# Second pass over the adjacency matrix: units of 16 rows with 1 KB runs in place of 8 rows with 2 KB runs

## The chip, the core and the metric

One core of one Trainium2 chip runs the whole kernel. The metric is device time in microseconds for one execution; lower is better. The engines are TensorE (PE, matrix products), VectorE (DVE), ScalarE (ACT), GpSimd (POOL) and SyncE (SP, which here only issues DMAs). Sixteen DMA engines move data between HBM and SBUF (128 partitions); SP and ACT each have one hardware queue on all sixteen, called q1 (SP) and q10 (ACT) in the trace, and GpSimd has q0.

## The reference, cut to what matters

`x` is 8192 x 64, `adj` is 8192 x 8192 (256 MiB in float32), sparse in its values but stored densely.

```python
x = layernorm(x + 1 - 0.1 * x - 0.01 * sum(x * (adj @ x), axis=1))   # first layer
A = adj - diag(adj)
node_support = concat[(A > 0) @ h, (A < 0) @ h]                      # second layer, h = x
edge_output  = gru(node_support, h)
att          = softmax(where(A > 0, e_plus, where(A < 0, e_minus, NEG_INF)))
node_output  = gru((att * A) @ (h @ W), h)
x = layernorm(h + diag(adj) * edge_output + diag(adj) * node_output)
```

The attention logits depend on the row alone, so a row needs two sums over the matrix: `A @ h` and `(A > 0) @ h`, and the number of positive entries.

## The kernel before

The matrix is read twice. The **first pass** (class `First`, up to about 690 us) reads strips of 128 rows x 2048 columns with runs of 8 KB and computes the first layer. The **second pass** (class `Fast`) needs the matrix transposed, columns on the partitions, and is what the change touches. A third path, `Full`, runs only if a check of the signs at the end finds negative entries; with these inputs it does not run.

The second pass goes through K = 16 blocks of 512 rows. The 128 partitions are four groups of 32, and each group holds a quarter of the columns (2048), cut into 64 chunks of 32 columns. A block arrives in U = 8 units of 2 MB. A unit of the kernel before is 16 chunks (512 columns of each group, runs of 2 KB) x 256 of the 512 rows, so 8 rows on each partition; units 2w and 2w+1 are the two row halves of the same columns. Four units fit into `ring`. A unit takes four DMAs of 512 KB, one for each group: SP issues groups 0 and 1 (partitions 0 to 63), ACT issues groups 2 and 3 (`load_unit`, line 243).

For each unit POOL multiplies the diagonal of the block out (`no_diagonal`, L757, 256 elements on each partition). DVE then transposes 32 x 32 squares from `ring` into `at` (`turn`, L871). There are H = 16 transpositions in a block, each of 2048 elements on each partition, counted here from 0 to 15. One of them takes the 8 rows of eight chunks; numbers 0 and 2 read unit 0, numbers 1 and 3 read unit 1, numbers 4 and 6 unit 2, and so on. ACT makes the mask of each (`sign`, L998, `mask`<-`at`). PE multiplies in pairs: the weighed products of halves 2p and 2p+1 (`weigh`, L1078, reading `at`), then their mask products (`add`, L1090, reading `mask`); here a half is four chunks x 512 rows. So both transpositions and both masks of a pair must be there before its first product. `at` and `mask` hold two pairs.

Order on the queues. SP waits on the count of transpositions and then issues its two DMAs; `freed` (L257) gives the count: units 4, 5, 6, 7 are loaded after 3, 4, 7, 8 transpositions of the block, and units 0 to 3 of the next block after 11, 12, 15, 16. ACT issues its two DMAs behind the masks of halves 2, 3, 6, 7, 10, 11, 14, 15. Between SP's loads stands the store of an earlier block's result (L789, 128 KB in runs of 256 B); POOL loads 128 KB of rows in such runs in each block (L820).

Row-wise work for the block before is spread over the block: products on PE between the pairs (L1099 to L1138), gates and copies on ACT (L1008 to L1038), vector work on DVE (L878 to L952), and one power on POOL (L814), which stands ahead of the first unit's diagonal of the next block. ACT copies PE's sums out at the seam between blocks (L1008, L1009) behind the mask of half 0, and PE's first product of the block waits for that copy.

Of the kernel before, what the change touches and what calls it, by code (L numbers as in the profile page):

```python
# [5 lines left out]
P = 128  # L6
Q = 32
# [37 lines left out]
def build_gnn(nc, x, adj, w_gat, a_gat, w_ih_e, w_hh_e, b_ih_e, b_hh_e, w_ih_n, w_hh_n, b_ih_n, b_hh_n, out):  # L45
# [18 lines left out]
    UC = 16  # L64
    SLOTS = 4
    HC = 4
    RH = BANK // Q // 2
    U = 2 * (C // UC)
# [174 lines left out]
def load_unit(eng, b, prefix, k, v, groups=(0, 1, 2, 3)):  # L243


    RH, UC, GQ, slot = b["RH"], b["UC"], b["GQ"], v % b["SLOTS"]
    wide, rows = v // 2, v % 2
    raw = unit_view(b, slot).rearrange("p (f m) -> p f m", f=RH)
    for g in groups:
        eng.dma_start(  # L250
            raw[Q * g:Q * g + Q, :, :],
            b["adj"][bass.ds(k * BANK + rows * (RH * Q), RH * Q),
                     GQ * g + UC * Q * wide:GQ * g + UC * Q * (wide + 1)].rearrange(
                "(f ii) m -> ii f m", ii=Q)).then_inc(b["s_raw"][prefix][slot], 16)


def freed(v):  # L257


    return 4 * (v // 2) + v % 2 - 5  # L260
# [5 lines left out]


def pair_view(t, pair):

    at = 2 * (pair % 2)  # L270
    return t[:, at:at + 2, :, :].rearrange("p s c i -> p (s c) i")
# [477 lines left out]
def no_diagonal(nc, pool, b, prefix, k, u):  # L749

    U, UC, RH, SLOTS = b["U"], b["UC"], b["RH"], b["SLOTS"]
    start = (u % 2) * RH * Q
    raw = unit_view(b, u % SLOTS)[:, start:start + Q]
    diag = bass.AP(tensor=raw.tensor, offset=raw.offset, ap=[list(raw.ap[0]), [UC * Q + Q, RH], [1, Q]])
# [4 lines left out]
        in1=b["not_diag"][:, bass.ds(k + (U // 2 - 1 - u // 2), 1), :].to_broadcast([P, RH, Q]), op=ALU.mult)  # L759
# [6 lines left out]
class Fast:  # L766
# [15 lines left out]
    def sync(self, sp):  # L782
# [9 lines left out]
        def block(k, first, old):  # L792
            for u in range(slots if first else 0, U):

                sp.wait_ge(s["turned"], k * (2 * U) + freed(u))
# [51 lines left out]
    def vector(self, dve):  # L847
        nc, b, s, ps = self.nc, self.b, self.s, self.b["ps"]
        H, HC, RH = self.H, b["HC"], b["RH"]
# [9 lines left out]
        def turn(k, half, first):  # L859
            n = k * H + half  # L860
            pair, rows = half // 2, half % 2
            v = 2 * (pair // 2) + rows
# [6 lines left out]
            raw = unit_view(b, v % b["SLOTS"]).rearrange("p (f c q) -> p f c q", f=RH, q=Q)  # L869
            to = pair_view(b["at"], pair)[:, :, RH * Q * rows:RH * Q * (rows + 1)]  # L870
            nc.vector.transpose(  # L871
                to.rearrange("p c (f q) -> p f c q", q=Q),
# [650 lines left out]
```

## Time and profile before

| | us |
|---|---|
| median of 3 runs (1623.57 to 1632.53) | 1627.84 |
| the profiled execution | 1620.43 |
| its span, first to last instruction | 1618.8 |
| PE busy in the span | 1418.2 (88%) |
| DVE busy | 1375.8 (85%) |
| ACT busy | 1180.4 (73%) |
| POOL busy | 191.7 (12%) |

Times in the rows are counted from the start of the span. HBM delivered 543.56 MB in all, on average 338 GB/s. The mean granted TensorE clock was 0.977 of full speed. A line such as `L871 DVE STREAM_TRANSPOSE at<-ring` is line 871 of the kernel, its engine, its operation, and the tile written and read.

### The profile page before, as it was taken

The page shows a single profiled execution, that of the slowest core. Times are in us where ns is not written, and L with a number is a line of the kernel's source. Part 1 is how long each engine was busy: PE and PEld are TensorE (multiplying, and loading weights), DVE is VectorE, ACT ScalarE, POOL GpSimd, SP SyncE. Part 2 cuts the span into 40 slices and gives each one's busy share as a digit, 9 for nine tenths or more (in the row PEclk, how much of TensorE's full clock was granted, in tenths as well). Part 3 has the DMA queues.
Part 4 walks back from the last instruction along what each step waited for, and adds up shares of the span by engine and source line. Part 5 has one row for each costly group of instructions (what it writes and reads, how often), then busy time and mean ns, then how long its engine had stood idle before and what let it go on. Part 6 is the DMA issues. An engine that isn't in the chain of part 4 may idle for free.

```text
span 1618.8 us, 22381 instructions
## 1 busy us (share of the span) xinstructions
PE 1418.2 (88%) x6262; PEld 786.5 (49%) x6262; DVE 1375.8 (85%) x1335; ACT 1180.4 (73%) x1427; POOL 191.7 (12%) x243
## 2 busy tenths in 40 slices
PE   7988888888888888659999999999999999999995
PEld 6655555555555555424444444444444444444442
DVE  4999999999999999777878888888887888889883
ACT  5988888888888888656666667666666766676662
POOL 3001010101010101031111101110111111011100
PEclk9999999999999999979999999999999999999996
DMA  9999999999999999999999999999999999999970
GB/s 270 405 422 421 410 421 411 421 410 420 412 421 411 421 411 421 355 307 338 313 285 278 321 311 305 302 321 310 285 318 309 307 297 313 311 304 301 322 208 11
DMA packets 216970, 548.08 MB, mean 339 GB/s; under 512 B 52336, under 2 KB 52352, under 8 KB 184176
## 3 DMA queue, kind: packets, MB, share of 16 engines
q1 hardware_dynamic: 127280, 405.87, 70.0%
q10 hardware_dynamic: 88320, 138.95, 29.3%
q0 software_dynamic: 1344, 2.99, 0.7%
q14 instruction: 19, 0.16, 0.0%
q8 instruction: 7, 0.11, 0.0%
HBM read 543.56 MB, written 4.19 MB: 338 GB/s over the span
## 4 chain that ended last, share of the span: by engine, by line
PE 44%; DVE 21%; DMA 20%; issue 12%; ACT 1%; DVEq 1%; POOL 1%; ACTq 0%; SPq 0%; POOLq 0%
PE ps L1078 23%; DMA ring<-in_adj 20%; DVE ps L645 17%; PE ps L1090 12%; DVE at L871 3%; PE ps L607 2%; PE ps L1124 2%; PE ps L574 1%; PE ps L1129 1%; PE ps L1107 1%; PE ps L1119 1%; PE ps L1099 1%; PE ps L1114 1%; PE ps L1138 1%; ACT final L1009 0%
## 5 line engine op out<-in xcount | busy, mean ns | idle before, releaser
L998 ACT ACTIVATE mask<-at 128x2048 fp32r<-128x2048 uint32 x256 | 489.4, 1912 | 288.6 <-DVE at L871 287.2
L871 DVE STREAM_TRANSPOSE at<-ring 128x2048 f32<-128x2048 f32 x256 | 582.6, 2297 | 114.0 <-PE ps L1078 57.0
L607 PE MATMUL ps<-mask,parts 128*128 128x512 f32 x2048 | 543.1, 407 | 107.4 <-DVE ps L645 101.8
L645 DVE SCALAR_TENSOR_TENSOR ps<-ring,ps 128x2048 f32<-128x2048 f32 x256 | 585.8, 2299 | 51.6 <-DMA ring<-in_adj 34.8
L529 ACT ACTIVATE at<-ring 128x2048 bf16<-128x2048 f32 x256 | 489.2, 1911 | 92.4 <-DMA ring<-in_adj 87.6
L1078 PE MATMUL ps<-at,hk 128*64 128x512 f32 x2048 | 478.9, 604 | 56.5 <-ACT final L1009 30.0
L607 PEld LDWEIGHTS ps<-mask,parts 128*128 128x128 f32 x2048 | 366.0, 188 | 284.6 <-DVE ps L645 215.9
L1078 PEld LDWEIGHTS ps<-at,hk 128*64 128x64 f32 x2048 | 147.6, 138 | 306.2 <-issue 261.6
L1090 PE MATMUL ps<-mask,parts 128*128 128x512 f32 x1024 | 269.4, 405 | 5.9 <-issue 5.9
L1090 PEld LDWEIGHTS ps<-mask,parts 128*128 128x128 f32 x1024 | 182.3, 188 | 143.7 <-issue 103.1
L757 POOL TENSOR_TENSOR ring<-ring,not_diag 128x256 f32<-128x256 f32 x128 | 94.5, 738 | 551.1 <-DMA ring<-in_adj 550.7
L433 POOL TENSOR_TENSOR at<-at,lsum 128x512 f32<-128x512 f32 x7 | 7.3, 1045 | 430.9 <-DVE lsum L662 430.9
L998 ACT ACTIVATION_READ_ACCUMULATOR mask<-at (+1 forms) x256 | 47.8, 187 | 0.0
L529 ACT ACTIVATION_READ_ACCUMULATOR at<-ring 128x1 f32 x256 | 47.7, 186 | 0.0
L814 POOL TENSOR_TENSOR ls<-ls,power 128x4 f32<-128x4 f32 x16 | 16.5, 1033 | 232.2 <-DVE ls L947 232.2
L1124 PE MATMUL ps<-final,w_edge 128*64 128x512 f32 x64 | 36.1, 648 | 2.6 <-DVE final L911 2.6
L1125 PE MATMUL ps<-final,w_node 128*64 128x512 f32 x64 | 36.1, 648 | 0.0
L645 DVE DVE_READ_ACCUMULATOR ps<-ring,ps (+1 forms) x256 | 36.1, 141 | 0.0
L918 DVE SCALAR_TENSOR_TENSOR final<-final 128x512 f32<-128x512 f32 x16 | 11.1, 696 | 24.2 <-ACT final L1030 19.0
L621 DVE TENSOR_TENSOR mask<-ps,mask 64x512 fp32r<-64x512 f32 x16 | 11.1, 695 | 14.1 <-ACT mask L486 14.1
L574 PE MATMUL ps<-ident,final 128*64 128x128 f32 x256 | 17.1, 305 | 6.8 <-DMA final<-in_x 6.8
L1124 PEld LDWEIGHTS ps<-final,w_edge 128*64 128x64 f32 x64 | 6.4, 140 | 29.9 <-issue 25.7
(155 smaller groups left out, 669.2 us busy)
## 6 DMA issues: line engine op xcount, KB each, us to landing
ring<-in_adj SPq DMA_DIRECT2D x256, 1024.0 KB, 17.4
ring<-in_adj SPq DMA_DIRECT2D x256, 512.0 KB, 10.3
ring<-in_adj ACTq DMA_DIRECT2D x256, 512.0 KB, 11.8
stage<-h_rows POOLq DMA_DIRECT2D x16, 128.0 KB, 6.6
out<-final SPq DMA_DIRECT2D x16, 128.0 KB, 13.3
h_rows<-final ACTq DMA_DIRECT2D x7, 256.0 KB, 22.9
hk<-h_rows ACTq DMA_DIRECT2D x7, 256.0 KB, 23.9
final<-in_x ACTq DMA_DIRECT2D x2, 512.0 KB, 10.1
```

The lines of the kernel that those rows point to most:

```text
L529: nc.scalar.activation(signs[:, unit % 2, :], ring[:, unit % RING, :], ACT.Sign, accum_out=row_signs[:, unit:unit + 1]).then_inc(s["signs_ ...
L574: last = nc.tensor.matmul(ps[D * half:D * half + D, q % 4, P * i:P * i + P], xn[:, 4 * q + i, :], ident[:], start=True, stop=True, skip_gr ...
L607: last = nc.tensor.matmul(ps[:, 4 * (n % 2) + i, :], pair[:, t % 2, e, :], x2[:, cols], start=e == 0, stop=e == 1)
L645: nc.vector.scalar_tensor_tensor(out=gram, in0=ring[:, i % RING, :], scalar=1.0, in1=gram, op0=ALU.mult, op1=ALU.mult, accum_out=flat[:, b ...
L757: return nc.gpsimd.tensor_tensor(out=diag, in0=diag, in1=b["not_diag"][:, bass.ds(k + (U // 2 - 1 - u // 2), 1), :].to_broadcast([P, RH, Q ...
L814: nc.gpsimd.tensor_tensor(out=b["ls"][:, 3, :], in0=b["ls"][:, 2, :], in1=b["power"][:, 0:4], op=ALU.pow).then_inc(s["rstd_ready"], 1)
L871: nc.vector.transpose(to.rearrange("p c (f q) -> p f c q", q=Q), raw[:, :, 2 * HC * (pair % 2):2 * HC * (pair % 2 + 1), :]).then_inc(s["tu ...
L998: nc.scalar.activation(pair_view(b["mask"], half // 2)[:, :, cols], pair_view(b["at"], half // 2)[:, :, cols].bitcast(U32), ACT.Sign, accu ...
L1078: last = mm(o, h[:, c, :], b["at"][:, half % 4, cl, :], start=c < 2, stop=c >= H * HC - 2)
L1090: last = mm(ps[:, ACC_S, :], parts[:, c, :], b["mask"][:, half % MS, cl, :], start=c == 0, stop=c == H * HC - 1)
L1124: mm(ps[lo, bank, :], b["w_edge"][:, t, :], sums, start=True, stop=True)
L1125: mm(ps[hi, bank, :], b["w_node"][:, t, :], wsum, start=True, stop=True, skip_group_check=True).then_inc(s["gates"], 1)
```

## The change

A unit becomes 8 chunks (256 columns of each group, runs of 1 KB) x all 512 rows, so 16 rows on each partition. It is still 2 MB in four DMAs of 512 KB. A transposition takes 16 rows of four chunks, which is exactly one half of PE's products; numbers 2u and 2u+1 read unit u. SP loads units 4 to 7 after 2, 4, 6, 8 transpositions, and so on evenly; ACT behind each odd half. PE waits for one transposition (one mask) ahead of the products of a half, no longer for both of a pair. The buffers `at` and `mask` are freed half by half. The order of instructions on each engine is otherwise the same. `Full` is changed in the same way.

```diff
-    UC = 16
+    UC = 8
+    U = C // UC
-    HC = 4
-    RH = BANK // Q // 2
-    U = 2 * (C // UC)
+    HC = UC // 2
@@ load_unit
-    raw = unit_view(b, slot).rearrange("p (f m) -> p f m", f=RH)
+    raw = unit_view(b, slot).rearrange("p (f m) -> p f m", f=RB)
-            b["adj"][bass.ds(k * BANK + rows * (RH * Q), RH * Q),
-                     GQ * g + UC * Q * wide:GQ * g + UC * Q * (wide + 1)].rearrange(
+            b["adj"][bass.ds(k * BANK, BANK), GQ * g + UC * Q * u:GQ * g + UC * Q * (u + 1)].rearrange(
                 "(f ii) m -> ii f m", ii=Q)).then_inc(b["s_raw"][prefix][slot], 16)
-def freed(v):
-    return 4 * (v // 2) + v % 2 - 5
@@ no_diagonal
-    start = (u % 2) * RH * Q
-    diag = bass.AP(..., ap=[list(raw.ap[0]), [UC * Q + Q, RH], [1, Q]])
+    raw = unit_view(b, u % SLOTS)[:, (u % 2) * UC * (UC * Q):(u % 2 + 1) * UC * (UC * Q)]
+    diag = bass.AP(..., ap=[list(raw.ap[0]), [UC * Q + Q, UC], [1, Q]])
@@ Fast.sync
-                sp.wait_ge(s["turned"], k * (2 * U) + freed(u))
+                sp.wait_ge(s["turned"], k * (2 * U) + 2 * (u + 1 - slots))
@@ Fast.vector, turn
-            if pair % 2 == 0:
-                dve.wait_ge(s["diagonal_out"], k * self.U + v + 1)
+            if part == 0:
+                dve.wait_ge(s["diagonal_out"], k * self.U + u + 1)
-                dve.wait_ge(s["weighed_done"], n - rows - 2)
-                dve.wait_ge(s["mask_ready"], n - rows - 2)
+                dve.wait_ge(s["weighed_done"], n - 3)
+                dve.wait_ge(s["mask_ready"], n - 3)
-                to.rearrange("p c (f q) -> p f c q", q=Q),
-                raw[:, :, 2 * HC * (pair % 2):2 * HC * (pair % 2 + 1), :])
+                b["at"][:, half % 4, :, :].rearrange("p c (f q) -> p f c q", q=Q),
+                raw[:, :, HC * part:HC * part + HC, :])
@@ Fast.scalar, sign
-                act.wait_ge(s["added_done"], n - half % 2 - 2)
+                act.wait_ge(s["added_done"], n - MS + 1)
-            u = 2 * (half // 4 + 2) + half % 2
-            if half % 4 >= 2 and (u < U or not last):
+            u = half // 2 + SLOTS
+            if half % 2 == 1 and (u < U or not last):
                 load_unit(act, b, "f_", k + u // U, u % U, (2, 3))
@@ Fast.tensor
-            pe.wait_ge(s["turned"], k * H + half - half % 2 + 2)
+            pe.wait_ge(s["turned"], k * H + half + 1)
-            pe.wait_ge(s["mask_ready"], k * H + half - half % 2 + 2)
+            pe.wait_ge(s["mask_ready"], k * H + half + 1)
```

## Rows read from the trace of the kernel before

**Rows 1.** Chain of waits by time, 850 to 1600 us: start, length, what.
```profile
868.92 5.35 PE ps L1078 x16
...
925.28 3.65 PE ps L1078 x16
...
980.37 3.65 PE ps L1078 x16
...
1035.43 3.65 PE ps L1078 x16
```
**Rows 2.** Busy time by engine, one block; then granted clock, DMA share, GB/s.
```profile
980.37:1035.43 55.06, 52.55 (x246) 24.88 (x247) 46.47 (x47) 37.46 (x44) 7.67 (x10) 1.00 1.06 308
```
**Rows 3.** Timeline of the seam: start, length, engine, line, idle before, releaser.
```profile
1027.65 1.03 POOL L814 TENSOR_TENSOR ls<-ls,power 128x4 f32<-128x4 f32 x1 [13.98 <-DVE ls L947]
...
1029.59 2.31 DVE L871 STREAM_TRANSPOSE at<-ring 128x2048 f32<-128x2048 f32 x1 [2.02 <-PE ps L1078]
...
1034.72 0.58 ACT L1009 COPY final<-ps 64x512 f32<-64x512 f32 x1
```
**Rows 4.** The chain of waits, 700 to 1600 us, longest pieces.
```profile
745.69 17.56 DMA ring<-in_adj
774.19 15.20 DMA ring<-in_adj
...
813.79 21.18 DMA ring<-in_adj
```
**Rows 5.** Groups by line and shape: count, busy us, mean ns, idle before.
```profile
L871 DVE STREAM_TRANSPOSE at<-ring 128x2048 f32<-128x2048 f32 x203 | 462.6, 2298 | 79.9 <-PE ps L1078 52.6 <-POOL ring L757 22.5 <-ACT mask L998 3.0
L998 ACT ACTIVATE mask<-at 128x2048 fp32r<-128x2048 uint32 x203 | 388.1, 1912 | 225.1 <-DVE at L871 223.8
...
L757 POOL TENSOR_TENSOR ring<-ring,not_diag 128x256 f32<-128x256 f32 x101 | 74.2, 735 | 424.0 <-DMA ring<-in_adj 423.7
```
**Rows 6.** DMA in that block: packets by size, then each queue's share.
```profile
DMA packets 9247, 16.99 MB, mean 308 GB/s; under 512 B 1050, under 2 KB 1050, under 8 KB 9247
...
q1 hardware_dynamic: 4855, 8.47, 53.6%
q10 hardware_dynamic: 4344, 8.38, 51.3%
```
**Rows 7.** Busy time as in rows 2: 8 KB runs, 256 B, 2 KB, 2 KB, two blocks.
```profile
620.00:630.00 10.00, 8.40 (x34) 5.64 (x33) 9.87 (x11) 8.80 (x11) 2.69 (x2) 1.00 1.01 421
4.00:7.00 3.00, 0.21 (x2) 0.24 (x4) 0.00 (x0) 1.28 (x1) 3.00 (x6) 1.00 1.35 220
958.00:967.00 9.00, 9.00 (x46) 5.02 (x43) 8.37 (x6) 4.87 (x6) 0.74 (x1) 1.00 1.06 365
...
820.00:828.00 8.00, 8.00 (x48) 4.42 (x47) 7.40 (x14) 6.26 (x9) 0.74 (x1) 1.00 1.09 238
757.00:835.00 78.00, 73.87 (x358) 36.72 (x358) 61.64 (x67) 51.57 (x61) 10.35 (x13) 1.00 1.06 307
```
**Rows 8.** DMA queues from 990.7 to 994.1 us: packets, MB, share.
```profile
DMA packets 771, 0.85 MB, mean 246 GB/s; under 512 B 406, under 2 KB 406, under 8 KB 771
q10 hardware_dynamic: 387, 0.75, 93.1%
q1 hardware_dynamic: 384, 0.10, 17.4%
```
**Rows 9.** Timeline of the second pass's start.
```profile
697.21 4.53 POOL L459 TENSOR_TENSOR parts<-hk,parts 128x2048 fp32r<-128x2048 f32 x1
697.30 2.31 DVE L871 STREAM_TRANSPOSE at<-ring 128x2048 f32<-128x2048 f32 x1 [2.10 <-POOL ring L757]
...
701.69 0.72 POOL L757 TENSOR_TENSOR ring<-ring,not_diag 128x256 f32<-128x256 f32 x1
...
704.91 5.74 PE L1078 MATMUL ps<-at,hk 128*64 128x512 f32 x16 [25.53 <-DVE at L871]
```
**Rows 10.** Timeline of ACT: one ordinary DMA issue of 1024 packets, two slow ones.
```profile
661.23 0.34 ACTq L298 DMA_DIRECT2D hk<-h_rows  x1
...
675.08 3.16 ACTq L250 DMA_DIRECT2D ring<-in_adj  x1
...
688.94 2.60 ACTq L250 DMA_DIRECT2D ring<-in_adj  x1
```
**Rows 11.** Timeline: PE's first weighed products of blocks 1 and 2.
```profile
753.04 3.65 PE L1078 MATMUL ps<-at,hk 128*64 128x512 f32 x16 [1.02 <-DVE at L871]
...
809.62 3.65 PE L1078 MATMUL ps<-at,hk 128*64 128x512 f32 x16 [2.68 <-ACT final L1009]
```

More of the change, by code:

```diff
@@ L240, in _, with load_unit @@
                 full.vector(dve)
-def load_unit(eng, b, prefix, k, v, groups=(0, 1, 2, 3)):
-    RH, UC, GQ, slot = b["RH"], b["UC"], b["GQ"], v % b["SLOTS"]
-    wide, rows = v // 2, v % 2
-    raw = unit_view(b, slot).rearrange("p (f m) -> p f m", f=RH)
+def load_unit(eng, b, prefix, k, u, groups=(0, 1, 2, 3)):
+    RB, UC, GQ, slot = b["RB"], b["UC"], b["GQ"], u % b["SLOTS"]
+    raw = unit_view(b, slot).rearrange("p (f m) -> p f m", f=RB)
     for g in groups:
@@ L860, in turn @@
             n = k * H + half
-            pair, rows = half // 2, half % 2
-            v = 2 * (pair // 2) + rows
-            if pair % 2 == 0:
-                dve.wait_ge(s["diagonal_out"], k * self.U + v + 1)
+            u, part = half // 2, half % 2
+            if part == 0:
+                dve.wait_ge(s["diagonal_out"], k * self.U + u + 1)
             if not (first and half < 4):
-                dve.wait_ge(s["weighed_done"], n - rows - 2)
-                dve.wait_ge(s["mask_ready"], n - rows - 2)
-            raw = unit_view(b, v % b["SLOTS"]).rearrange("p (f c q) -> p f c q", f=RH, q=Q)
-            to = pair_view(b["at"], pair)[:, :, RH * Q * rows:RH * Q * (rows + 1)]
+                dve.wait_ge(s["weighed_done"], n - 3)
+                dve.wait_ge(s["mask_ready"], n - 3)
+            raw = unit_view(b, u % b["SLOTS"]).rearrange("p (f c q) -> p f c q", f=RB, q=Q)
             nc.vector.transpose(
-                to.rearrange("p c (f q) -> p f c q", q=Q),
-                raw[:, :, 2 * HC * (pair % 2):2 * HC * (pair % 2 + 1), :]).then_inc(s["turned"], 1)
+                b["at"][:, half % 4, :, :].rearrange("p c (f q) -> p f c q", q=Q),
+                raw[:, :, HC * part:HC * part + HC, :]).then_inc(s["turned"], 1)
         def weighed_sum(k, c):
@@ L993, in sign @@
             if not (first and half < MS):
-                act.wait_ge(s["added_done"], n - half % 2 - 2)
-            cols = slice(RH * Q * (half % 2), RH * Q * (half % 2 + 1))
+                act.wait_ge(s["added_done"], n - MS + 1)
             nc.scalar.activation(
-                pair_view(b["mask"], half // 2)[:, :, cols], pair_view(b["at"], half // 2)[:, :, cols].bitcast(U32),
-                ACT.Sign, accum_out=b["seen"][:, bass.ds(n, 1)]).then_inc(s["mask_ready"], 1)
-            u = 2 * (half // 4 + 2) + half % 2
-            if half % 4 >= 2 and (u < U or not last):
+                b["mask"][:, half % MS, :, :].rearrange("p c i -> p (c i)"),
+                b["at"][:, half % 4, :, :].rearrange("p c i -> p (c i)").bitcast(U32), ACT.Sign,
+                accum_out=b["seen"][:, bass.ds(n, 1)]).then_inc(s["mask_ready"], 1)
+            u = half // 2 + SLOTS
+            if half % 2 == 1 and (u < U or not last):
                 load_unit(act, b, "f_", k + u // U, u % U, (2, 3))
@@ L1191, in sync @@
             if u >= slots:
[L1192 removed]
+                sp.wait_ge(s["turned"], 2 * (u + 1 - slots))
             load_unit(sp, b, "g_", 0, u)
@@ L1218, in turn @@
             n = k * H + half
-            wide, part = half // 4, half % 4
+            u, part = half // 2, half % 2
             if part == 0:
-                dve.wait_ge(s["diagonal_out"], k * self.U + 2 * wide + 2)
-            raw = b["ring"][:, 4 * (wide % 2):4 * (wide % 2) + 4, :].rearrange("p r m -> p (r m)").rearrange(
-                "p (f c q) -> p f c q", f=RB, q=Q)
+                dve.wait_ge(s["diagonal_out"], k * self.U + u + 1)
+            raw = unit_view(b, u % b["SLOTS"]).rearrange("p (f c q) -> p f c q", f=RB, q=Q)
             nc.vector.transpose(
```

17 lines of the change are left out of this document (6 added, 11 removed).

## The prediction

> **What bounds the kernel now.** I read three views in this order: the chain of waits of the second pass, the busy time of one block, and the DMA queues in that block. The chain shows where the blocks begin: PE's first weighed products come at 925.28, 980.37 and 1035.43 us, so a block lasts 55.1 us [rows 1]. The block from 868.92 lasts 56.4, with products of 5.35 us for 3.65. In a block PE is busy 52.55 of 55.06 us, DVE 46.47, ACT 37.46 [rows 2]. PE sets the pace. The 2.5 us that it lacks stand at the seam: POOL's power at 1027.65 delays the diagonal, transposition 0 comes at 1029.59, the mask follows, ACT's copy ends at 1035.30 and PE starts at 1035.43 [rows 1, 3].
>
> The reader should see a second limit close behind. In blocks 0 to 2 the chain runs through loads of the ring, 17.6, 15.2 and 21.2 us long [rows 4]. From 757 to 835 us the DMA brought 307 GB/s and PE had 73.87 of 78 us of work [rows 7]. In the later blocks 308 GB/s suffice, because PE asks for no more [rows 2]. So DMA is within a few per cent of being the bound, and the change doubles the number of its packets.
>
> **The change, part by part.** The sum is made against the profiled execution, 1620.43 us (span 1618.8). The median of the three runs is 1627.84, 7.4 us more; I add my difference to the median.
>
> *Work of the engines.* The transpositions stay at 16 a block with 2048 elements on each partition, mean 2298 ns; the masks too, 1912 ns; POOL's diagonal keeps 256 elements, 735 ns [rows 5]. Only strides change. I cost these at nothing. DVE has 8.6 us free in a block [rows 2], that is 0.54 us for each transposition before it would matter; a cheaper stride gains nothing while PE or DMA is the bound. The DMA instructions stay at 16 a block on each queue; a DMA of 1024 packets was issued in 0.34 us [rows 10], so 512 packets in place of 256 cost no issue time by themselves.
>
> *Waits.* PE asks for one transposition instead of two. At the seam this gives nothing: PE waits there for ACT's copy (L1009) [rows 3], which stands behind the mask of half 0, transposition 0, POOL's diagonal and the power, all in the same order after the change. In the block PE hardly waits for a transposition. DVE may write into `at` one half earlier; of its 79.9 us of idle time from 850 to 1550 us, 52.6 are put down to PE [rows 5], but PE stays the slower engine, so this is slack. Loads get one transposition more of lead: unit 4 is released after 2 and needed by number 8 (before: 3 and 8), unit 5 after 4, needed by number 10 (before: 4 and 9). With 55.06 / 16 = 3.4 us for each, six periods of lead, 20.6 us, take the place of five, 17.2.
>
> *The start.* Transposition 1 no longer needs the second unit. It can follow number 0 (697.30, 2.31 us long) at 699.6; before, it waited for POOL's diagonal at 701.69 and came at 702.45. PE needs only number 0 and can start at about 699.7 for 704.91 [rows 9]. That is 5 us; the mask products behind it wait for POOL's low parts (L459), ready at 701.74, and that is covered by the 5.7 us of weighed products. I take -4.
>
> *Packets.* With 16 engines, the time from one packet to the next on an engine is 16 x size / rate. With both queues loaded the rows give: 256 B at 220 GB/s, 18.6 ns; 2 KB at 365 GB/s, 89.8 ns; 8 KB at 421 GB/s, 311 ns [rows 7]. No row shows 1 KB. A straight line from 256 B to 2 KB gives 18.6 + 768/1792 x 71.2 = 49.1 ns; the slope from 2 KB to 8 KB, (311.3 - 89.8) / 6144 x 1024 = 36.9 ns, leads back from 89.8 to 52.9 ns; the cheap end is half of 89.8, 44.9 ns, and the dear end is the whole 18.6 of a small packet on top of 36.9, 55.5 ns. I take 49.1, between its two neighbours, which is 334 GB/s.
>
> A block has 16384 packets of 1 KB, 1024 on each engine: 50.3 us (46.0 at the cheap end, 56.8 at the dear end). Its 1050 small packets [rows 6] add 66 x 18.6 ns = 1.2 us. Before, it was 512 x 89.8 ns = 46.0, and 1.2: 47.2 of 55.1 us. The other 7.9 us are lost where one queue has little to give and the rate falls to 238 GB/s [rows 7]. Such a stretch loses 1 - 238/365 = 35% of its time, so they are about 23 us of a block.
>
> How much of these stays decides. Two things shorten them: loads are released evenly and not two at a time, and the 256 B packets of the store hold up less. While the store is in SP's queue the two queues deliver packet for packet (384 and 387), so SP's queue brings 0.10 MB and ACT's 0.75 [rows 8]; with 1 KB packets the same number of turns moves half as much on ACT's side. At 334 GB/s a stretch of 238 loses 29%. If all 23 us stay, a block needs 50.3 + 1.2 + 6.6 = 58.1 us; if half of them stay, 54.8. I take the middle, 56.4 us, 1.3 over PE's 55.1. Two chains so near each other, coupled by three units, also wait for each other: from 757 to 835 us both PE (95% busy) and DMA ran near their limits [rows 7]. I put 0.5 us a block on that.
>
> *Sum.* Blocks 3 to 14 are twelve: 12 x (1.3 + 0.5) = 21.6 us; the last block prefetches nothing, 0.7. Blocks 0 to 2 were held by DMA already and keep their time, 0. The start gives -4. Together +18 us: 1638.7 for the profiled execution, 1646 for the median.
>
> *Two rules of the Trainium skill.* The 2 KB packets of this trace reach 365 GB/s where 8 KB reach 421 [rows 7]. "DMA: Bandwidth & Descriptors" (Specifications) puts the smallest transfer for full rate at 512 B, by which 1 KB would cost no more than 2 KB a byte; the rate of 2 KB speaks against it here, and by that rule the packets of a block stay at 46.0 us and the sum has no DMA term, which is the first two rivals below. "Advanced Engine Details and Errata" (Clock Domains) gives 42 to 43 ns for an unobstructed 1 KiB descriptor; as an estimate that is 43.5 us a block for the 50.3 above, and it too speaks against my slowdown. No row here shows a 1 KB packet.
>
> **The rivals.**
> *DMA keeps up, and nothing is won.* If half or more of the one-queue stretches go and 1 KB costs 49 ns or less, a block needs 54.8 us or less and PE's 55.1 stay. For it speaks the longer lead (20.6 for 17.2 us); against it, that blocks 1 and 2 were late with 2 KB [rows 4]. The start's gain is eaten in blocks 0 to 2, where loads are still the bound: 0 to +5 us, median 1630.
> *The other side: the release order was what held the early blocks.* Its place is blocks 0 to 2. Block 1 began at 753.04 us, block 2 at 809.62 [rows 11], block 3 at 868.92 [rows 1], so they lasted 56.6 and 59.3 us for 55.1. If even releases keep both queues filled, 1.5 + 4.2 = 5.7 us go there, and 4 at the start: -10 us, median 1618. It decides from the point at which a block's DMA work falls under 55 us in blocks 1 and 2 too. For it speaks that the rate is 365 whenever both queues give [rows 7].
> *Issues that block ACT.* Two DMA issues of ACT took 3.16 and 2.60 us [rows 10], when its queue held the packets of some four DMAs; twice the packets may bring this into every unit. Eight more waits of 2.5 us are 20 us a block, ACT has 17.6 free [rows 2], so 2.4 over, and 2.8 with its effect on the masks: 13 x 2.8 - 4 = +32 us, median 1660. Against it: such an issue stands behind the start of a mask of 1.9 us, which covers most of it.
> *The dear packet.* At 55.5 ns a block needs 56.8 + 1.2 + 4 to 6 = 62 to 64 us: 13 x 7 to 9 = +91 to +117 us, median about 1730. For it speaks only that rows 32 KB apart are read in shorter pieces; no row shows it.
>
> **How the numbers follow.** My forecast gets 0.40, with 1634 to 1662 as its own range (1 KB at 47 to 52.9 ns). DMA keeps up: 0.24. The other side: 0.14. Blocked issues: 0.10. The dear packet: 0.12. Half a per cent is 8 us, about what can be told from no change here. Faster is the other side alone, 0.14. Within 0.5% is the second case and the low end of the first, 0.26. Slower is the rest, 0.60. The range of 8 in 10 goes from 1616 to 1690; outside it lie the dear packet and half of the tail below.
>
> **What would show it.** Right: a period of 56 to 57 us between the first weighed products of blocks, the chain of waits going through `ring<-in_adj` in the later blocks, DMA around 300 GB/s, and 320 to 345 GB/s in stretches where both queues give equally. Each step: PE's first product near 700 us; transpositions of 2.3 us and masks of 1.9 as before. Wrong: a period of 55.1 with idle loads (the packet cost or the one-queue stretches were overrated), transpositions that take longer than 2.8 us (the stride was not free), or ACT's DMA issues of 2 to 3 us in each block.

## The result, and the profile after

The changed kernel takes 1803.19 us (median of 4 runs, 1791.93 to 1821.64) against 1625.8 us for the kernel before in the same comparison: a ratio of 1.108, 95% interval 1.103 to 1.113. It is slower, as forecast, but by 177 us and not by 18. Ratios here and below leave out a kernel's slowest, disturbed runs, so they need not be the quotient of two medians.

| | before | after |
|---|---|---|
| span of the profiled execution, us | 1618.8 | 1791.8 |
| PE busy, us | 1418.2 (88%) | 1481.3 (83%) |
| DVE busy, us | 1375.8 | 1382.6 |
| ACT busy, us | 1180.4 | 1182.2 |
| HBM, GB/s over the span | 338 | 306 |

The groups of the engines, by line and shape (columns as in [rows 5], here over the whole span), show the same cost of a transposition (2299 ns), a mask (1911) and a diagonal (744). What grew is the idle time ahead of them: over the whole span it was 114.0 us ahead of DVE's transpositions before and is 252.8 now, 288.6 and 428.2 ahead of the masks, 551.1 and 801.9 ahead of POOL's diagonals. Its source is the ring's DMA:

```profile
L852 DVE STREAM_TRANSPOSE at<-ring 128x2048 f32<-128x2048 f32 x256 | 583.9, 2299 | 252.8 <-POOL ring L740 232.8 <-PE ps L1059 10.4 <-ACT mask L978 6.1
L978 ACT ACTIVATE mask<-at 128x2048 fp32r<-128x2048 uint32 x256 | 489.2, 1911 | 428.2 <-DVE at L852 388.7 <-PE ps L1071 20.6 <-issue 17.3
L740 POOL TENSOR_TENSOR ring<-ring,not_diag 128x256 f32<-128x256 f32 x128 | 95.2, 744 | 801.9 <-DMA ring<-in_adj 801.8
```

Busy time by engine (columns as in [rows 2]) shows where the time is lost: everywhere in the second pass, and in the rate of the DMA. The first row is early, the second covers 600 us of steady blocks (the last three numbers of a row are the granted clock, the DMA share and GB/s):

```profile
750.00:850.00 100.00, 79.05 (x357) 37.45 (x359) 66.02 (x69) 53.88 (x64) 10.68 (x14) 0.93 1.12 249
900.00:1500.00 600.00, 513.00 (x2192) 232.16 (x2190) 413.93 (x409) 333.44 (x381) 67.76 (x87) 0.93 1.12 251
```

The same 600 us of the kernel before:

```profile
900.00:1500.00 600.00, 573.18 (x2675) 271.24 (x2673) 504.37 (x502) 407.02 (x466) 82.94 (x108) 0.99 1.05 307
```

PE's busy time over the span grew by 63 us though its products are the same: its granted clock in these 600 us is 0.93, where it was 0.99. The blocks do not wait for it: PE is busy 513 of these 600 us.

At 251 GB/s the 16.99 MB of a block [rows 6] take 67.7 us, 12.6 more than the 55.1 of [rows 1]. POOL's power, one for each block, confirms the period: 65.3 and 67.6 us.

```profile
1236.68 1.03 POOL L797 TENSOR_TENSOR ls<-ls,power 128x4 f32<-128x4 f32 x1 [7.94 <-DVE ls L928]
1301.99 1.03 POOL L797 TENSOR_TENSOR ls<-ls,power 128x4 f32<-128x4 f32 x1 [7.93 <-DVE ls L928]
1369.58 1.03 POOL L797 TENSOR_TENSOR ls<-ls,power 128x4 f32<-128x4 f32 x1 [7.94 <-DVE ls L928]
```

The DMA share is 1.12, more than before, at a lower rate: the DMA engines are occupied longer for each byte. The DMA queues show when. From 1254 to 1258 us both queues give equally, 334 GB/s at 1 KB packets; from 1263 to 1266 ACT's q10 gives nearly all, 214 GB/s; from 1268 to 1272 it is SP's q1, 213 GB/s (columns as in [rows 8]):

```profile
DMA packets 1357, 1.34 MB, mean 334 GB/s; under 512 B 51, under 2 KB 1357, under 8 KB 1357
q1 hardware_dynamic: 675, 0.67, 55.7%
q10 hardware_dynamic: 682, 0.67, 55.2%
...
DMA packets 641, 0.64 MB, mean 214 GB/s; under 512 B 15, under 2 KB 641, under 8 KB 641
q10 hardware_dynamic: 602, 0.60, 105.8%
q1 hardware_dynamic: 39, 0.04, 6.8%
...
DMA packets 873, 0.85 MB, mean 213 GB/s; under 512 B 44, under 2 KB 873, under 8 KB 873
q1 hardware_dynamic: 777, 0.76, 101.3%
q10 hardware_dynamic: 96, 0.09, 11.6%
```

From these shares a packet occupies a DMA engine for 52 ns in the first stretch and for 84 ns in the second (16 engines x time x share / packets).

And the DMA issues changed. The view of the loading line from 900 to 1500 us gives for each queue: number of issues, shortest, median and longest in ns, first and last start. Before:

```profile
L250 SPq DMA_DIRECT2D ring<-in_adj x172: 316/317/602, 912.4 to 1496.3; - x172
```

After:

```profile
L247 SPq DMA_DIRECT2D ring<-in_adj x142: 316/3598/7122, 897.5 to 1498.2; - x142
L247 ACTq DMA_DIRECT2D ring<-in_adj x142: 322/384/5266, 900.4 to 1498.8; - x142
```

SP now spends 3.6 us on an issue that took 0.32 (here called a stall); ACT does not. These stalls stand in the chain of waits from 900 to 1700 us, which now leads through SP's issues and the loads (before, from 900 to 1500 us, PE's products of L1078 and L1090 took 49.2% and 25.9% of it):

```profile
by line: SPq L247 37.2%; DMA ring<-in_adj 36.8%; issue 14.1%; SPq L772 4.3%; DVE at L852 4.3%; POOL ring L740 2.1%; DVE final L933 0.4%; DVE final L907 0.2%; DVE final L906 0.2%; SPq L778 0.1%; DVEq L849 0.1%; DVE final L918 0.1%; DVE final
```

The timeline of these issues (start, length) reads, SP first, then ACT:

```profile
1257.41 3.61 SPq L247 DMA_DIRECT2D ring<-in_adj  x1
1261.27 2.88 SPq L247 DMA_DIRECT2D ring<-in_adj  x1
1264.33 3.95 SPq L247 DMA_DIRECT2D ring<-in_adj  x1
...
1258.61 0.86 ACTq L247 DMA_DIRECT2D ring<-in_adj  x2
1266.31 0.32 ACTq L247 DMA_DIRECT2D ring<-in_adj  x1
```

Read with the queues: ACT's two, through by 1259.5, are moved alone from 1263 to 1266. SP's two, through at 1261.0 and 1264.2, are moved alone from 1268 to 1272. Then ACT's of 1266 follow. The DMAs are moved in the order in which their issue ended, over both queues together. This was counted for every load from 900 to 1500 us, with the median time of its packets. Taken are one DMA of SP and one of ACT whose issues ended more than 1 us apart and whose packets lie within 15 us of each other. In the changed kernel all but a few of 934 such couples, 1.00, were moved in the order of issue; before it was 1.00 of 1131. Many of these couples lie far apart, so the close ones say more: of the 160 in the changed kernel whose issues ended 1 to 3 us apart, 158 kept the order. The difference: before, 2% of SP's loads had no issue of ACT within 1 us; after, 69%. Call two loads that are issued within 1 us of each other in step.

### The profile page after: what moved, and what is told of

Read it like the earlier page. It is cut to its first block, busy times and chain, and to the rows that moved or that the text cites. A ratio compares the mean times of both kernels' runs of the same rounds, so it can differ in the third digit from the quotient of the medians.

```text
span 1791.8 us, 22613 instructions
## 1 busy us (share of the span) xinstructions
PE 1481.3 (83%) x6262; PEld 799.9 (45%) x6262; DVE 1382.6 (77%) x1335; ACT 1182.2 (66%) x1427; POOL 192.4 (11%) x243
## 4 chain that ended last, share of the span: by engine, by line
SPq 21%; DMA 20%; issue 12%; DVE 4%; POOL 2%; ACTq 2%; ACT 1%; POOLq 0%; DVEq 0%; PE 0%
DMA ring<-in_adj 20%; SPq L247 19%; DVE at L852 3%; SPq L772 2%; ACTq L247 1%; POOL ring L740 1%; ACT mask L978 1%; POOL parts L443 0%; DVE final L933 0%; DVE final L907 0%; DVE final L906 0%; ACT at L513 0%; PE ps L1119 0%; POOL lsum L436 0%; DVE final L918 0%
## 5 line engine op out<-in xcount | busy, mean ns | idle before, releaser
L852 DVE STREAM_TRANSPOSE at<-ring 128x2048 f32<-128x2048 f32 x256 | 583.9, 2299 | 252.8 <-POOL ring L740 232.8
L978 ACT ACTIVATE mask<-at 128x2048 fp32r<-128x2048 uint32 x256 | 489.2, 1911 | 428.2 <-DVE at L852 388.7
L629 DVE SCALAR_TENSOR_TENSOR ps<-ring,ps 128x2048 f32<-128x2048 f32 x256 | 586.1, 2299 | 51.0 <-DMA ring<-in_adj 38.2
L1059 PE MATMUL ps<-at,hk 128*64 128x512 f32 x2048 | 520.2, 647 | 96.9 <-ACT final L990 67.3
L513 ACT ACTIVATE at<-ring 128x2048 bf16<-128x2048 f32 x256 | 489.3, 1911 | 94.2 <-DMA ring<-in_adj 82.1
L1059 PEld LDWEIGHTS ps<-at,hk 128*64 128x64 f32 x2048 | 156.4, 148 | 381.5 <-issue 292.7
L740 POOL TENSOR_TENSOR ring<-ring,not_diag 128x256 f32<-128x256 f32 x128 | 95.2, 744 | 801.9 <-DMA ring<-in_adj 801.8
L1119 PE MATMUL ps<-two,final 128*128 128x64 f32 x128 | 22.3, 330 | 38.8 <-DVE final L908 38.8
L1119 PEld LDWEIGHTS ps<-two,final 128*128 128x128 f32 x128 | 19.7, 235 | 46.3 <-DVE final L908 46.3
```

What stands on the lines that cost most here:

```text
L513: nc.scalar.activation(signs[:, unit % 2, :], ring[:, unit % RING, :], ACT.Sign, accum_out=row_signs[:, unit:unit + 1]).then_inc(s["signs_ ...
L629: nc.vector.scalar_tensor_tensor(out=gram, in0=ring[:, i % RING, :], scalar=1.0, in1=gram, op0=ALU.mult, op1=ALU.mult, accum_out=flat[:, b ...
L740: return nc.gpsimd.tensor_tensor(out=diag, in0=diag, in1=b["not_diag"][:, bass.ds(k + (U // 2 - 1 - u // 2), 1), :].to_broadcast([P, UC, Q ...
L852: nc.vector.transpose(b["at"][:, half % 4, :, :].rearrange("p c (f q) -> p f c q", q=Q), raw[:, :, HC * part:HC * part + HC, :]).then_inc( ...
L978: nc.scalar.activation(b["mask"][:, half % MS, :, :].rearrange("p c i -> p (c i)"), b["at"][:, half % 4, :, :].rearrange("p c i -> p (c i) ...
L1059: last = mm(o, h[:, c, :], b["at"][:, half % 4, cl, :], start=c < 2, stop=c >= H * HC - 2)
```

## The experiments

"Before" is rerun on the same chip in each comparison. The packets of an experiment are those of the kernel it starts from, unless said.

**The packets themselves (e1_narrow, e2_more_dmas).** The kernel before, with each DMA cut in two:

```diff
 e1_narrow (before; diagonal and transposition read the new order)
+        for h in range(2):
+            at = GQ * g + UC * Q * wide + UC // 2 * Q * h      # 256 columns: 1 KB
+            eng.dma_start(raw[Q * g:Q * g + Q, h, :, :], b["adj"][rows, at:at + UC // 2 * Q] ...)
 e2_more_dmas (before)
+        for h in range(2):                                     # 4 of the 8 rows: 2 KB
+            eng.dma_start(raw[Q * g:Q * g + Q, RH // 2 * h:RH // 2 * (h + 1), :], ...)
```

> The kernel before, with nothing changed but the packets: each DMA of 256 packets of 2 KB is cut into two of 256 packets of 1 KB (the unit lies in the ring as two column halves). Order of release, transpositions and waits are those of before. Queue theory (each queue takes only about 1000 packets ahead, both are fed by one generator, so with 1 KB packets the queues run dry in turn): ratio to before 1.08 to 1.12, DMA about 250 GB/s in the second pass, many DMA issues of 2 to 8 us. Rival A (packets of 1 KB are slow in themselves, 64 ns or more): the same ratio, but 250 GB/s also where both queues give equally. Rival B (the new order of release and the new transpositions cost the time): ratio 1.00 to 1.02.

> Control for the first: the kernel before with each DMA cut into two of 128 packets of 2 KB (four rows each). As many DMA instructions as in the first, half the packets. Queue theory, if what fills a queue is packets: ratio 0.99 to 1.01. If what fills it is the number of DMA instructions: ratio 1.05 or more.

Measured: e1_narrow 1629.81 us, ratio 1.0014 (0.9968 to 1.0061); e2_more_dmas 1.0041 (1.0012 to 1.0071). In e1_narrow, 344 GB/s where both queues give, 308 over the 600 us:

```profile
1244.00:1249.00 5.00, 5.00 (x28) 2.99 (x26) 4.93 (x5) 2.79 (x3) 0.00 (x0) 1.00 1.11 344
900.00:1500.00 600.00, 573.25 (x2668) 269.83 (x2668) 509.97 (x504) 410.68 (x470) 83.48 (x109) 0.99 1.11 308
```

So neither the 1 KB packet nor the doubled number of packets or DMAs costs more than 0.7% here, the upper ends of the two intervals.

**The size of a DMA, and a throttle (e3_split, e4_throttle).** Both on the changed kernel:

```diff
 e3_split: each DMA of 512 packets becomes two of 256, 8 rows each
 e4_throttle, SP only
+                sp.wait_ge(b["s_raw"]["f_"][(u - 2) % slots], <unit u-2 has landed>)
                 load_unit(sp, b, "f_", k, u, (0, 1))
```

> The changed kernel with each DMA of 512 packets cut into two of 256 packets of 1 KB (eight rows each). Queue theory with packets as what fills a queue: still 1.08 to 1.11 over before, perhaps 0.01 better than the changed kernel since a blocked DMA holds the generator for a shorter time. If it is the 512 packets of one DMA that block: 1.00 to 1.04.

> The changed kernel, and SP waits before each unit until the unit two before it has landed, so that its queue never holds much more than 1024 packets. Queue theory with one generator for both queues: SP no longer blocks it while ACT's queue runs dry, so the one-queue stretches shrink and the ratio falls from 1.11 to 1.04 to 1.09. Rival A (1 KB packets slow in themselves) and a theory of too little work outstanding: no better than 1.11, rather 1.12 to 1.15, since less is on its way.

Measured: 1765.71 us, 1.0845 (1.0801 to 1.0889), and 1872.95 us, 1.1486 (1.1421 to 1.1552). The size of a DMA is worth 0.02 of the 0.11. The throttle took nearly all stalls from SP and made the kernel slower still, 234 GB/s:

```profile
L247 SPq DMA_DIRECT2D ring<-in_adj x132: 316/336/2603, 900.7 to 1494.3; - x132
```

So taking the stalls away is no cure by itself, and my theory that fewer outstanding packets of SP cure it fell. The wait also moved SP's issues away from ACT's: 64% had none of ACT within 1 us. It made SP's loads later as well, so this run alone does not tell which of the two cost the time.

**The release of the slots (e5_pairs, e6_aligned, e7_even, e8_pairs_split).**

```diff
 e5_pairs (after): released as before, in pairs
-                sp.wait_ge(s["turned"], k * (2 * U) + 2 * (u + 1 - slots))
+                sp.wait_ge(s["turned"], k * (2 * U) + 2 * (u + 1 - slots) + (u + 1) % 2)
-            u = half // 2 + SLOTS
-            if half % 2 == 1 and ...
+            u = 2 * (half // 4 + 2) + half % 2
+            if half % 4 >= 2 and ...
 e6_aligned (after)
-                sp.wait_ge(s["turned"], ...
+                sp.wait_ge(s["mask_ready"], ...
 e7_even (before): SP waits for freed(u) + 1 + u % 2, ACT loads unit half // 2 + 3 at each odd half
 e8_pairs_split: e5_pairs and e3_split together
```

> The changed kernel, with one thing put back: slots come free in pairs, as in the kernel before. SP loads units at turned counts 3, 4, 7, 8 of each group of eight instead of 2, 4, 6, 8, and ACT after signs 2, 3, 6, 7 instead of 1, 3, 5, 7. Release theory (the even release makes SP issue ahead of ACT, the two queues get out of step and run one at a time): both-queue stretches come back, 300 GB/s and more in the second pass, ratio 0.99 to 1.02. Address theory (the order in which the 1 KB pieces lie in memory, all 512 rows of 256 columns, is what slows them, and the release has no part in it): stays at 1.09 to 1.12. Plain lateness theory (an odd slot's unit comes one turn later than it could): 1.12 or more.

> The changed kernel, where SP waits for the mask of the half (mask_ready) instead of its transposition (turned), so that SP issues its half of a unit in the same moment as ACT, about 2.5 us later than now. Skew theory (SP's head start over ACT lets the queues alternate): rate goes to 290 GB/s or more, ratio 1.00 to 1.04, and SP's issues fall from 3.46 us to about 0.35. Address theory: no gain, 1.10 to 1.13. Even-release theory (the spacing of the releases itself, not the skew): no gain, 1.10 to 1.13.

> The kernel before with the release made even and nothing else: SP loads units at turned counts 4, 6, 8, 10 instead of 3, 4, 7, 8, ACT after signs 3, 5, 7, 9. Its 2 KB packets, its tiling and its transpositions stay. Release theory: slower, 1.04 to 1.11, rate in the second pass falls to 260 to 280 GB/s with one-queue stretches. Address theory: 0.99 to 1.02 (the units come one or two turns later, which costs up to 1 us per block).

> e5_pairs with each DMA of 512 packets cut in two of 256 (8 rows each). If the size of a DMA adds its own cost (it was 0.023 in the even release) this is 0.01 to 0.03 below e5_pairs. Release theory: 0.99 to 1.01, level with the narrow pieces in the tiling of before (1.001). Address theory: 1.07 to 1.09, as the split kernel with the even release.

Measured: e5_pairs 1637.19 us, 1.0069 (1.0038 to 1.0101). e8_pairs_split 1625.68 us, 0.9995 (0.9963 to 1.0028). e7_even 1654.05 us, 1.0155 (1.0116 to 1.0195). e6_aligned 1834.05 us, 1.1291 (1.1229 to 1.1353). Two edited conditions take back 0.10 of the 0.11: the release counts are the cause. With those counts, tiling, packets, strides and waits of PE together are worth 0.007, which the smaller DMAs bring to nothing. That an even release is bad by itself is refuted by e7_even, which lost a seventh of it. My expectation for e6_aligned rested on a mistake: ACT's issue does not wait for the end of its mask. In the changed kernel it began within 0.3 us of the mask's start for 45 of the 71 units between 900 and 1500 us, 1.6 to 3.7 us behind it for the others. So SP and ACT were for the most part scheduled to the same moment already, and the wait for the mask's end put SP behind ACT (median 2.9 us, with 74% of SP's issues without one of ACT within 1 us).

**Later, but still even (e9_one_later, e10_two_later, e11_narrow_even).**

```diff
 e9_one_later (after): SP "+ 1"; ACT loads unit half // 2 + 3 at even halves
 e10_two_later (after)
+                sp.wait_ge(s["turned"], k * (2 * U) + 2 * (u + 1 - slots) + 2)
+            u = half // 2 + SLOTS - 1
+            if half % 2 == 1 and not (first and half == 1) and ...
 e11_narrow_even: e1_narrow with the release of e7_even
```

> The changed kernel with the even release kept and made one turn later for both queues: SP at turned counts 3, 5, 7, 9, ACT after signs 2, 4, 6, 8. Backlog theory (it is not the evenness, but that an early release keeps three units, 1536 packets, in each queue; above about 1000 a queue's issues stall and the queues deliver one at a time at 210 to 240 GB/s; a release that comes when less is queued avoids it): a good part of the loss goes, 1.01 to 1.06. Evenness theory (single units released at equal distances are the harm, however much is queued): stays at 1.09 or more, plus nothing.

> The same, two turns later: SP at 4, 6, 8, 10, ACT after signs 3, 5, 7, 9; no more than two units beyond the one in use are ever in a queue (1024 packets). Backlog theory: 1.00 to 1.03, SP's issues near 0.32 us, over 300 GB/s where both queues hold packets. Evenness theory: 1.09 or more. Plain lateness theory (buffers come free later, so transfers start later): above the one-turn kernel, 1.12 or more.

> The tiling and transpositions of the kernel before, 1 KB packets in DMAs of 256 (as the narrow kernel, 1.001), and the even release of the kernel e7 (SP at 4, 6, 8, 10, ACT after signs 3, 5, 7, 9), which with 2 KB packets gave 1.0155. At its release no more than two units are in flight. Backlog theory: 1.01 to 1.03. Evenness theory (1 KB packets with single releases are the harm): 1.07 to 1.10, as the changed kernel.

Measured: e9_one_later 1646.0 us, 1.0126 (1.009 to 1.0162); e10_two_later 1632.99 us, 1.0019 (0.9994 to 1.0043); e11_narrow_even 1680.82 us, 1.0331 (1.0299 to 1.0363). The same transfers, started two transpositions (7 us) later, bring back what the change lost. In e10_two_later the stalls are gone and 1% of SP's loads stand without one of ACT within 1 us:

```profile
L247 SPq DMA_DIRECT2D ring<-in_adj x169: 316/348/1233, 899.6 to 1497.5; - x169
L247 ACTq DMA_DIRECT2D ring<-in_adj x169: 322/384/538, 899.7 to 1497.7; - x169
```

```profile
900.00:1500.00 600.00, 564.93 (x2587) 263.81 (x2587) 496.59 (x484) 395.56 (x455) 82.40 (x107) 0.98 1.10 301
```

Evenness is not the harm. e11_narrow_even came in just above the 1.01 to 1.03 of the backlog theory. Its queues are in step. Counted from the program, its units are released 4 and 3 transpositions ahead of the one that needs them (in e10_two_later always 4, in the kernel before always 5); that this shorter lead is what it lost is argued, not shown.

The 1536 and 1024 packets of my expectations are miscounted, since a queue gets 1024 packets of a unit and not 512. In the traces, when SP began an issue, the packets that it had already issued and that had not started numbered 1074 in the changed kernel (median, 900 to 1500 us), 846 in e9_one_later and 600 in e10_two_later.

**One queue moved at a time (e14_sp_later, e15_act_later, e17_skew).** On the changed kernel: SP two turns later, ACT unchanged; ACT two later, SP unchanged; SP one later and ACT two.

> The changed kernel with SP alone two turns later (turned counts 4, 6, 8, 10); ACT stays at signs 1, 3, 5, 7. SP's queue then holds at most two units, ACT's three, and SP issues about 7 us behind ACT. In-step theory (each queue must be given the same unit at the same moment; when one falls behind, stretches with one giving queue at 220 GB/s follow): as bad as the changed kernel or worse, 1.08 to 1.15. Theory that the backlog in SP's queue, whose issues stall, is the harm: 1.00 to 1.04. Theory that the backlog in ACT's queue is the harm: 1.07 or more.

> The other way round: ACT alone two turns later (after signs 3, 5, 7, 9), SP as in the changed kernel. In-step theory: 1.08 to 1.15. Theory of SP's backlog: 1.07 or more, SP's issues still near 3 us. Theory of ACT's backlog: 1.00 to 1.04.

> The changed kernel with SP one turn later and ACT two turns later. Both in step gave 1.0126 (one turn) and 1.0019 (two turns); here the backlog lies between the two and ACT issues its half of a unit one turn, about 3.4 us, behind SP. In-step theory: clearly slower than both, 1.04 to 1.10, with one-queue stretches. Backlog theory (only the amount queued counts): 1.00 to 1.02.

Measured: e14_sp_later 1671.17 us, 1.0259 (1.022 to 1.0299). e15_act_later 1809.18 us, 1.1119 (1.1055 to 1.1183). e17_skew 1812.75 us (1769.89 to 1844.06) beside 1631.08, too far apart for an interval: 1.085 to 1.131 times. The issues of SP, e14_sp_later:

```profile
L247 SPq DMA_DIRECT2D ring<-in_adj x172: 316/336/1950, 900.5 to 1498.9; - x172
```

e15_act_later:

```profile
L247 SPq DMA_DIRECT2D ring<-in_adj x143: 316/3584/7675, 894.7 to 1495.5; - x143
```

e17_skew:

```profile
L247 SPq DMA_DIRECT2D ring<-in_adj x140: 316/1774/6209, 903.9 to 1499.7; - x140
```

These three cut both of my theories down as I had put them; the theory of SP's backlog held for the first two and missed the third. e14_sp_later gives the queues different units, yet at the same moment (SP unit 4 at the count at which ACT loads unit 5), and is nearly cured: being on the same unit does not matter. e15_act_later shares the moments too, but SP is still released three units ahead, its issues stall for 3.6 us, and the moments drift apart. e17_skew holds less backlog than e9_one_later in ACT's queue and the same in SP's, but is scheduled a turn apart, and loses 0.085 or more where e9_one_later lost 0.013. So two loads issued at the same moment are what matters. That backlog does harm by way of SP's stalls, which pull the queues out of step, fits all of these runs. The share of SP's loads from 900 to 1500 us whose issue ended over 1 us away from any of ACT's splits the fifteen kernels of the table: at 0.36 or less the ratio is 1.033 at most, at 0.49 or more it is 1.085 at least:

| kernel | share | ratio |
|---|---|---|
| e11_narrow_even, e7_even | 0.00 | 1.033, 1.016 |
| e10_two_later, before, e14_sp_later | 0.01, 0.02, 0.03 | 1.002, 1, 1.026 |
| e1_narrow, e8_pairs_split | 0.07, 0.09 | 1.001, 1.000 |
| e9_one_later, e5_pairs | 0.19, 0.36 | 1.013, 1.007 |
| e3_split | 0.49 | 1.085 |
| e4_throttle, e15_act_later, e17_skew | 0.64, 0.66, 0.69 | 1.149, 1.112, 1.085 to 1.131 |
| after, e6_aligned | 0.69, 0.74 | 1.108, 1.129 |

In all of them 0.96 to 1.00 of the couples were moved in the order of issue.

Within the two groups the share does not order the ratios (e5_pairs has 0.36 and 1.007). A second count is closer to what costs the time: the share of 1 us slices, 900 to 1500 us, in which one queue brought over 85% of the bytes of both. It is 0.38 in the changed kernel and 0.31 to 0.57 in the other five of the slow group; it is 0.23 at most in the rest, 0.13 in e10_two_later, 0.04 in e1_narrow. The 0.23 is the kernel before: there such slices cost nothing that can be seen, since e1_narrow with 0.04 is no faster.

**Why a DMA alone is slow (e18_spread, e19_one_queue).** SP issues everything; in e18_spread one DMA takes one block of 32 rows for all 128 partitions:

```diff
+    for f in range(RB):
+        eng.dma_start(raw[:, f, :], b["adj"][bass.ds(k * BANK + f * Q, Q), :].rearrange(
+            "ii (g c) -> g ii c", g=G)[:, :, UC * Q * u:UC * Q * (u + 1)]).then_inc(...)
```

> The changed kernel (even, early release) where SP alone issues all loads and each DMA takes the 1 KB pieces of one block of 32 rows for all 128 partitions (128 packets; 16 DMAs a unit) instead of 512 packets for 32 partitions. Theory that DMAs are moved in the order of their issue, and that one DMA alone is slow because it writes only 32 partitions: a DMA of 128 partitions alone gives 300 GB/s or more, ratio 0.99 to 1.05 though only one queue is used. Theory that one queue alone can't give more than about 225 GB/s, whatever it writes: a block takes 16.8 MB / 225 GB/s = 75 us, ratio 1.15 to 1.22. SP needs 128 issues of 0.32 us, 41 us of a block.

> Control to the kernel above: SP alone issues all loads, in the changed kernel's DMAs of 512 packets for 32 partitions each, so that one DMA follows another and none has a partner. Both theories: one DMA at a time, 210 to 240 GB/s, 70 to 80 us a block instead of 56, ratio 1.15 to 1.25. A ratio of 1.05 or less would say that DMAs of one queue overlap among themselves, and that the order of issue does not explain the one-sided stretches.

Measured: e19_one_queue 1994.15 us, 1.2213 (1.2123 to 1.2303), as both theories had it, at 212 GB/s (its profile):

```profile
900.00:1500.00 600.00, 465.19 (x1838) 206.78 (x1838) 349.08 (x344) 281.23 (x321) 58.10 (x76) 0.87 1.13 212
```

e18_spread 3552.06 us, 2.1802 (2.1661 to 2.1944), which neither had: 97 GB/s with 28% of the DMA engines' time used and SP's issues at a median of 1.13 us.

```profile
DMA packets 10183, 9.73 MB, mean 97 GB/s; under 512 B 821, under 2 KB 10182, under 8 KB 10182
q1 hardware_dynamic: 10182, 9.72, 27.7%
```

A load with no partner costs what the stretches of the changed kernel cost. e18_spread does not decide between the single queue and the 32 partitions, since it met another limit. Its trace shows which: a packet took 46 ns (87 in e19_one_queue), but only 4 or 5 were under way at nearly every moment, 4.3 on average for 17.6. That looks like the work of about four DMA engines; as an estimate, 4.3 x 1024 B / 46 ns is 96 GB/s. The source of its DMAs has the four groups as its outermost dimension; that this is the reason is not shown.

The single queue is not the limit, and the trace of the kernel before shows it: the 421 GB/s of [rows 7], from 620 to 630 us, came through SP's queue alone, in DMAs of the first pass that write all 128 partitions in 8 KB packets.

```profile
DMA packets 579, 4.21 MB, mean 421 GB/s; under 512 B 65, under 2 KB 65, under 8 KB 65
q1 hardware_dynamic: 579, 4.21, 101.1%
```

Packet size does not fit as the reason either: alone, loads of 2 KB packets (before) and of 1 KB packets (after) ran at nearly the same rate, 230 and 218 GB/s in the slices counted above, where two queues reach 365 and 344. What is left, as far as these runs tell, is where the loads write or read. SP's loads write only partitions 0 to 63 and ACT's only 64 to 127, so a load in step always has a partner in the other half. In e19_one_queue the rate around the change from one DMA to the next is 226 and 232 GB/s where the next writes the other half (groups 1 to 2 and 3 to 0), and 213 and 211 where it does not. This points to the partitions; a load of 128 partitions with 1 KB packets on all DMA engines, which could prove it, was not run.

**A faster kernel (e12_seam, e13_seam_later).** POOL's power of block k moves behind the first diagonal of block k+2; e13_seam_later is that on e10_two_later.

```diff
             for u in range(self.U):
                 no_diagonal(nc, pool, b, "f_", k, u).then_inc(s["diagonal_out"], 1)
+                if late and u == 0:
+                    power(k - 2)
-        with pool.Fori(1, self.K) as k:
-            block(k, k - 1)
-            power(k - 1)
+        block(1, 0)
+        with pool.Fori(2, self.K) as k:
+            block(k, k - 1, True)
+        power(self.K - 2)
```

> A way to a faster kernel, apart from the change: the kernel before, where POOL raises the variances of block k to the power -0.5 behind the diagonal of unit 0 of block k+2 instead of ahead of it. In the seam between blocks POOL waited for DVE's variance, then did the power (1.0 us), and only then the diagonal (0.7 us) for which DVE's first transposition waits; PE had nothing for 2.1 us. Expected: 1 to 2 us per block, 14 seams, 15 to 30 us less, ratio 0.980 to 0.992. Rival: the loads are what is late at the seam, the diagonal waits for the unit anyway, ratio 0.995 to 1.005.

> Looks for the fastest: the changed kernel with the release two turns later for both queues (1.0019) and POOL's power moved behind the next block's first diagonal (0.9907 on the kernel before). If the two add up: 0.988 to 0.996. If the later release leaves the first unit of a block late, so that the seam waits for data: 0.997 to 1.003.

Measured: e12_seam 1611.11 us against 1629.76, 0.9907 (0.9877 to 0.9937), a little faster than both kernels; 18.7 us over 14 seams are 1.3 us each, of the 2 that DVE stood idle in [rows 3]. Its timeline has the diagonal ahead of the power:

```profile
1014.93 0.73 POOL L757 TENSOR_TENSOR ring<-ring,not_diag 128x256 f32<-128x256 f32 x1 [6.32 <-DMA ring<-in_adj]
1021.18 1.03 POOL L814 TENSOR_TENSOR ls<-ls,power 128x4 f32<-128x4 f32 x1 [5.52 <-DVE ls L950]
```

e13_seam_later gave 1622.38 us (1598.62 to 1629.54) against 1631.08; four runs so far apart don't tell whether the two add up.

## Why the prediction was wrong

*Direction and place: right.* DMA, close behind PE, became the bound; the loads of the ring are what POOL and then DVE wait for.

*Work of the engines: right.* 2299, 1911 and 744 ns for 2298, 1912 and 735 [rows 5].

*The start: right.* PE's first product came at 700.22 us, forecast 699.7, before 704.91 [rows 9]:

```profile
700.22 5.97 PE L1059 MATMUL ps<-at,hk 128*64 128x512 f32 x16 [19.96 <-DVE at L852]
```

*The packet: its price right, its effect wrong.* I took 49.1 ns from one packet to the next. The row of 344 GB/s gives 16 x 1024 / 344 = 47.6 ns, within the bounds. (I had read all three rows as both queues loaded; the 8 KB row is SP's queue alone, as shown above.) But my sum made a block need 56.4 us, and the same packets in e1_narrow cost 1.0014: the price did not reach the end. The rule of the Trainium skill that 512 B is enough for full rate ("DMA: Bandwidth & Descriptors", Specifications), which I weighed against my sum, came out right for the kernel's time, though not for the rate (344 against 365 GB/s at 2 KB [rows 7]). The 42 to 43 ns that the Trainium skill gives for an unobstructed 1 KiB descriptor ("Advanced Engine Details and Errata", Clock Domains) were not reached with both queues loaded; the 1 KB packets of e18_spread took 46 ns.

*"Two things shorten" the one-queue stretches: this is the step that failed.* I put 23 us of such stretches in a block, of which half or all would stay. In the 1 us slices they were 0.23 of a block of 55.1 us, about 13 us, and became 0.38 of 67.7, about 26: they doubled. (The row of 238 GB/s from which I had the 23 us is no such stretch: both queues gave there, 57.5% and 51.3% of the engines' time, and 507 of 1382 packets were under 512 B, as those of the store are.) An evener and earlier release was to fill the queues better. It did the opposite: with the earlier release SP's queue holds 1074 packets when SP issues, its issues stall, SP and ACT no longer issue together, and loads are moved one after another at 210 to 240 GB/s. From PE's first product to the end, sixteen blocks took 913.9 us before (704.91 to 1618.8) and 1091.6 after (700.22 to 1791.8), 11.1 us more each; I had 1.8 more in twelve of them. I had taken more lead for a gain without a price; the release counts alone, put back (e5_pairs), give 1.0069.

*"512 packets in place of 256 cost no issue time by themselves".* True of ACT (median 384 ns), wrong for SP, 3598 ns. The row that warned, issues of 3.16 and 2.60 us [rows 10], I used for a rival on the wrong queue: there I asked whether ACT's masks would be late, and not whether the two queues would part. SP computes nothing, so I gave its stalls no price; the runs put their price at what they do to the pairing.

*"Loads get one transposition more of lead".* I counted this in favour of the change. It is the harm: six transpositions of lead are 1.108, and four in the same kernel, one less than before, give 1.0019.

*Blocks 0 to 2 "keep their time".* They lost too: 249 GB/s from 750 to 850 us, where it was 307 from 757 to 835 [rows 7].

## What stays open

Why SP's issues stall and ACT's hardly do. They go with much queued, but no one number of packets divides stalled from quick issues over these kernels: e1_narrow, with smaller DMAs, has 1058 packets ahead of an issue of SP and issues in 0.32 us, the changed kernel has 1074 and takes 3.6. Whether a load alone runs at 210 to 240 GB/s because it writes 32 partitions; the traces point there. Why couples kept the order less well in e5_pairs (0.96) than elsewhere. And e7_even and e11_narrow_even are in step but 0.016 and 0.033 slower; that their later release in the tiling of before is the reason is argued, not shown.

## What to carry to other kernels

When two queues share a transfer, look in the trace at the moments of their issues and at each queue's packets in windows of a few us, not at the mean rate: two loads issued together, into different halves of the partitions, ran at 334 to 365 GB/s, alone at 210 to 240. Freeing a buffer earlier is not free; if it fills a queue until issues stall, releasing later can be the faster choice (1.108 to 1.0019 here, by two conditions). And price a stall on an engine that computes nothing by what it does to the order of the others.

## What the runs showed of the hardware

- Loads of two hardware queues were moved in the order in which their issues ended, across the queues: 1.00 of 1131 couples before, 1.00 of 934 after, with medians of 8.1 and 6.6 us from the end of the issue to the packets.
- 1 KB packets reach 344 GB/s with both queues loaded (e1_narrow, 1244 to 1249 us; 47.6 ns from one to the next on an engine), 2 KB 365 (before, 958 to 967 us).
- One queue with DMAs for 32 partitions gives 212 GB/s (e19_one_queue), at a DMA share of 1.13: a 1 KB packet takes 87 ns, and 54 where both queues give (after, 1254 to 1258 us). One queue with DMAs for 128 partitions and 8 KB packets gives 421 GB/s (before, 620 to 630 us).
- An issue of SP took 0.32 us with a median of 512 packets of 2 KB ahead of it in its queue (before), 3.6 us with 1074 of 1 KB (after).
- A DMA that ACT issues behind a mask does not wait for the mask's end: in the changed kernel 45 of 71 such issues began within 0.3 us of the start of a mask of 1.9 us (one of them: mask at 1258.44, issue at 1258.61).
- DMAs of 128 packets that cover 128 partitions give 97 GB/s, with SP's issue at a median of 1.13 us, the DMA engines 28% busy and 4.3 packets under way (e18_spread).
